# One program block from the merge of keys to the end, the loop's first image prepared amid the way back of positions, and 29 of 32 gather chunks ahead

## The reference, cut to what matters

```python
x = x + conv(_ln_c(x))            # x: (32, 64, 48, 48); 32 images of 2304 pixels, 64 channels
#   conv: s = relu(xn^T xn) ** 2 over the pixels of one image, out = s times a 1x1 projection g
t = _to_tokens(x)                 # 32 * 2304 = 73,728 tokens
t = t + ffn(_ln_t(t))
#   ffn, gates: h = x W_gat; edges (262,144) with random src, dst, and one loop edge for each token
#     e = leaky_relu(a_src[src] + a_dst[dst]);  softmax of e over the edges of each dst
#     agg[dst] = sum of alpha * h[src];  layernorm, mean over heads, top 2 of 4 experts
#   out = sum over experts of gate * (gelu(x W1 + b1) W2 + b2)
```

## Time and profile before

| what | us |
|---|---|
| median of 3 runs | 5424.05 |
| lowest and highest of them | 5416.19, 5426.34 |
| profiled execution, its own time | 5427.65 |
| its span from first to last instruction | 5425.8 |
| busy: PE, DVE, ACT, POOL | 3722.4, 3970.8, 3400.6, 2943.8 |

### The profile page before, as it was taken

How to read it: one execution, slowest core, us unless ns; L and a number is a source line. 1 busy time by engine, 2 the same in 40 slices (tenths; PEclk the granted TensorE clock), 3 DMA queues, 4 the chain that set the end, 5 groups by cost and what they waited for, 6 DMA issues and landing times.

```text
span 5425.8 us, 61836 instructions
## 1 busy us (share of the span) xinstructions
PE 3722.4 (69%) x18367; PEld 1256.6 (23%) x18367; DVE 3970.8 (73%) x5512; ACT 3400.6 (63%) x4285; POOL 2943.8 (54%) x2937
## 2 busy tenths in 40 slices
PE   4888988300499999999999999994000017777878
PEld 1223333100133333333333333331000002222222
DVE  8998988997466666666666655555888857777877
ACT  4777888202576767676676767674555536566666
POOL 6000000007777777777777777773777137666661
PEclk9999999655699999999999999996555558888889
DMA  7000100002112222222222222223555527999997
GB/s 264 23 24 20 29 20 21 11 16 59 36 39 58 45 55 53 48 53 47 56 45 54 54 47 50 46 45 103 176 170 168 188 71 144 142 162 155 154 166 139
DMA packets 332446, 441.38 MB, mean 81 GB/s; under 512 B 183193, under 2 KB 261916, under 8 KB 331500
## 3 DMA queue, kind: packets, MB, share of 16 engines
q1 hardware_dynamic: 209744, 288.12, 19.4%
q0 software_dynamic: 105536, 148.61, 16.5%
q10 hardware_dynamic: 16896, 1.18, 0.2%
HBM read 252.35 MB, written 166.47 MB: 77 GB/s over the span
## 4 chain that ended last, share of the span: by engine, by line
POOL 36%; issue 14%; DMA 14%; DVE 8%; PE 4%; ACT 1%; SPq 1%; DVEq 0%; POOLq 0%; ACTq 0%
POOL rows L1692 33%; DMA rows<-htab_d,idx 8%; DMA gs<-gates_d 4%; PE ye L1913 2%; PE up L1925 2%; DVE ms L2594 1%; POOL R L1750 1%; DMA gates_d<-GH 1%; DVE pairs L2601 1%; ACT GT L2087 1%; DVE AD L2460 1%; DVE AE L2454 1%; POOL got L1705 0%; DVE total L2603 0%; POOL nb L1707 0%
## 5 line engine op out<-in xcount | busy, mean ns | idle before, releaser
L1692 POOL DMA_INDIRECT rows<-htab_d,idx x2048 | 2135.1, 1043 | 802.0 <-issue 595.8
L2376 DVE SCALAR_TENSOR_TENSOR s<-gram,rel 128x1024 f32<-128x1024 f32 (+1 forms) x720 | 802.7, 1117 | 860.0 <-ACT rel L2042 850.3
L2042 ACT ACTIVATE rel<-gram 128x1024 f32<-128x1024 f32 (+1 forms) x1080 | 1009.6, 940 | 605.9 <-PE gram L1860 574.5
L1818 PE MATMUL acc<-s,gT 128*64 128x512 f32 (+1 forms) x4320 | 1075.3, 576 | 0.0
L1859 PE MATMUL gram<-hl 128*128 128x512 f16 (+1 forms) x2160 | 777.1, 365 | 117.9 <-DVE s L2376 93.1
L1860 PE MATMUL gram<-hl,lh 128*128 128x512 f16 (+1 forms) x2160 | 765.8, 360 | 0.0
L1750 POOL DMA_INDIRECT R<-seg_d,nidx x576 | 588.5, 1022 | 191.4 <-issue 165.8
L1913 PE MATMUL ye<-hid,w 128*64 128x384 f32 x1536 | 376.1, 569 | 273.0 <-DVE ms L2594 208.6
L1030 POOL IOTA slots<- 64x2048 int32 x1 | 1.8, 1833 | 975.4 <-POOLq L182 975.4
L2134 ACT ACTIVATE hid<-up,b1t 128x768 f32<-128x768 f32 x384 | 333.3, 899 | 269.3 <-PE up L1925 267.9
L1896 PE MATMUL tailsT<-ident,tails 128*20 128x128 f32 x24 | 5.3, 414 | 652.1 <-DVE tails L2482 652.1
(11 more groups left out here) (372 smaller groups left out, 5349.8 us busy)
## 6 DMA issues: line engine op xcount, KB each, us to landing
gs<-gates_d SPq DMA_DIRECT2D x64, 1024.0 KB
rows<-htab_d,idx POOLq DMA_INDIRECT x2048
seg_d<-state SPq DMA_DIRECT2D x32, 996.0 KB, 4.3
raw_d<-w_zeros POOLq DMA_DIRECT2D x48, 512.0 KB, 22.5
raw_d<-rows POOLq DMA_DIRECT2D x32, 768.0 KB, 3.6
tne<-tn_d SPq DMA_DIRECT2D x32, 576.0 KB, 6.6
x2e<-x_d SPq DMA_DIRECT2D x32, 576.0 KB, 9.8
out<-res SPq DMA_DIRECT2D x64, 256.0 KB
```

Source lines behind the costliest of these rows:

```text
L1692: pool.indirect_dma_start(out=n.rows[:, k % 2, j, :], out_offset=None, in_=n.htabx, in_offset=bass.IndirectOffsetOnAxis(ap=n.idx[:, g % 2, ...
L1818: last = pe.matmul(acc[(par + c) % 2][j * C:(j + 1) * C, 0:w], gT[:, par, 2 * k + j, :], s2[:, u % SLOTS, j * w:(j + 1) * w], start=k == 0 ...
L2042: act.activation(rel[:, t % RELS, 0:2 * w].rearrange("p (j x) -> p j x", j=2), gram[(par + t) % 2][:, :, 0:w], ACT.Relu, scale=1.0 / SPLIT ...
L2376: dve.scalar_tensor_tensor(halves(s2[:, t % SLOTS, 0:2 * w]), gram[(par + t) % 2][:, :, 0:w], 1.0 / SPLIT ** 2, halves(rel[:, t % RELS, 0: ...
```

## The change

- Merge and routing stand in one block: the five streams of `merge_nodes` become functions (`merge_sync` and so on) that `flow` calls first. The semaphores of POOL's gather become ones of the whole program.
- POOL's gather is a function of its own (`gather_rows`). Its first 48 gathers (`OPENING`) are issued in the merge stream, the others follow. SP loads the first two index tiles `idx` right behind the store of `gidx_d`. `need` is computed for each of the 32 chunks, not for 8 groups.
- `AHEAD` goes from 28 to 29 chunks and `PIECE` from 11 to 8.
- Image 8 is loaded, projected, scaled and transposed between steps 7 and 17 of the way back. The buffers that it uses come after a filler (`apart`, 48 KiB a partition), so that they don't lie on those of the routing; `routed` has three parts, not four.
- In the edge stage ACT raises `a_ends` behind `AE` and a new `a_got` behind `GT`; DVE waits for `a_got` ahead of the first use of `GT`, and POOL waits for `a_got`.
- POOL's subtraction on `pos` stands behind the last gather, not behind the repair scatter.

```diff
-    AHEAD = 28
-    PIECE = 11
-    EARLY = 10
-    IN_FLIGHT = 4
+    AHEAD = 29
+    PIECE = 8
...
+def gather_rows(pool, n, t0, t1):
+    GC, G, NK = n.GC, n.G, 4 * n.G
+    for t in range(t0, t1):
+        k, j = divmod(t, GC)
+        g, c = divmod(k, 4)
+        if j == 0:
+            need = pool.value_load(n.need[0:1, NK - 1 - k:NK - k], min_val=16, max_val=16 * n.B)
+            pool.wait_ge(n.o_hx, need)
+            pool.sem_inc(n.opened, 1)
+        if j == 0 and c == 0:
+            if g < 2:
+                pool.wait_ge(n.i_in[g], 16)
+            else:
+                pool.wait_ge(n.j_in[g % 2], 16 * (g // 2))
+        if j == 0 and k >= 2:
+            pool.wait_ge(n.raw_out[k % 2], 16 * (k // 2))
+        if t >= IN_FLIGHT:
+            pool.wait_ge(n.landed[t % IN_FLIGHT], 16 * (t // IN_FLIGHT))
+        pool.indirect_dma_start(out=n.rows[:, k % 2, j, :], out_offset=None, in_=n.htabx,
...
+        def merge_sync(sp):
             sp.wait_ge(v_ids, 1)
             sp.dma_start(n.gidx.rearrange("(p j) a -> p (j a)", p=P), big[0][:, 0, :].bitcast(I32)).then_inc(ids_out, 16)
+            sp.wait_ge(ids_out, 16)
+            for par in range(2):
+                sp.dma_start(n.idx[:, par, :, :], ids_of(n)[n.G - 1 - par]).then_inc(n.i_in[par], 16)
...
             pool.wait_ge(one_out, 16)
-
-        @block.tensor
-        def _(pe):
+            pool.wait_ge(v_need, 1)
+            gather_rows(pool, n, 0, OPENING)
...
         @block.sync
         def _(sp):
+            n.merge_sync(sp)
...
+            load(0, 0)
+            load(1, 1)
+            sp.wait_ge(n.a_hl, NTB * (FIRST + 1))
+            swap_halves(0)
             sp.sem_inc(moves_free, 1)
             sp.wait_ge(v_xpos, 1)
             sp.dma_start(n.xpos[0:n.M, :].rearrange("(p j) a -> p (j a)", p=NR), slots[0:NR, 0:EC]).then_inc(x_out, 16)
             sp.wait_ge(x_out, 16)
-            load(0, 0)
-            load(1, 1)
-            sp.wait_ge(n.a_hl, NTB * (FIRST + 1))
-            swap_halves(0)
...
             t = AHEAD * GC
-            gather(0, t)
+            gather_rows(pool, n, OPENING, t)
             pool.wait_ge(img_done, 1)
...
+            pool.wait_ge(p_in, 16)
+            pool.tensor_scalar(pos[:, :], pos[:, :], -1.0, 0.0, ALU.add, ALU.max).then_inc(n.m_rdy, 1)
             pool.wait_ge(v_fi, 1)
...
             pool.wait_ge(fix_out, 16 * G)
-            pool.wait_ge(p_in, 16)
-            pool.tensor_scalar(pos[:, :], pos[:, :], -1.0, 0.0, ALU.add, ALU.max).then_inc(n.m_rdy, 1)
...
                     last.then_inc(pe_route, 1)
-            pe.wait_ge(n.x_in[0], 64 * (FIRST // 2 + 1))
-            for i in range(NB):
-                pre(FIRST, 0, i)
-            for i in range(NTB):
-                turn(FIRST, i)
+                if turn_no == 0:
+                    pe.wait_ge(n.x_in[0], 64 * (FIRST // 2 + 1))
+                    for i in range(NB):
+                        pre(FIRST, 0, i)
+                if turn_no == 1:
+                    for i in range(NTB):
+                        turn(FIRST, i)
+            pe.wait_ge(a_route, routes_done[-1])
...
-                act.activation(AE[:, par, :, :], nb[:, par, :, HE + NH:HE + 2 * NH].rearrange("p j h -> p h j"), ACT.Copy)
-                act.activation(GT[:, par, :, :], got[:, par, ::-1, 0:HE + NH].rearrange("p j w -> p w j"), ACT.Copy).then_inc(a_ends, 1)
+                act.activation(AE[:, par, :, :], nb[:, par, :, HE + NH:HE + 2 * NH].rearrange("p j h -> p h j"), ACT.Copy).then_inc(a_ends, 1)
+                act.activation(GT[:, par, :, :], got[:, par, ::-1, 0:HE + NH].rearrange("p j w -> p w j"), ACT.Copy).then_inc(a_got, 1)
...
+                if i == 9:
+                    spread(FIRST)
+                if i == 11:
+                    scales(FIRST)
+                if i == 13:
+                    units(FIRST)
+                if i == 15:
+                    low(FIRST)
...
+                    dve.wait_ge(a_got, k + 1)
                     link(dve.tensor_tensor(ee[:, :, :], gt[:, HE:HE + NH, :], AD[:, :, 1:CE], ALU.add))
```

More of the change, by code:

```diff
@@ L28 @@
 MIRROR = 40959
+IN_FLIGHT = 4
+EARLY = 10
+OPENING = 48
+KEPT = 49152
 def chunks(n, size=512):
@@ L111, in kernel_program @@
         n.o_hx = sem("o_hx")
+        n.i_in = [sem("i_in0"), sem("i_in1")]
+        n.j_in = [sem("j_in0"), sem("j_in1")]
+        n.landed = [sem(f"landed{f}") for f in range(IN_FLIGHT)]
+        n.raw_out = [sem("raw_out0"), sem("raw_out1")]
+        n.opened = sem("opened")
         n.o_tn = sem("o_tn")
@@ L1260, in flow @@
         with ExitStack() as routing:
[L1261 to L1268, removed]
+            routed_ps = routing.enter_context(nc.psum_tensor("routed", [P, 3, 1024], F32))
         vr = im_sb("vr", [P, QT, C])
         gT = im_sb("gT", [P, 2, QT, C])
[L1271 to L1278, removed]
         rel = im_sb("rel", [P, RELS, 1024])
@@ L1294, in flow @@
         step_t = im_sb("step_t", [P, W], U8)
+        apart = im_sb("apart", [P, KEPT // 4])
+        xh = im_sb("xh", [P, 2, HALF])
+        cv = im_sb("cv", [P, QT, 2 * C])
+        sq = im_sb("sq", [P, QT, C])
+        tk = im_sb("tk", [P, QT, C])
+        tw = im_sb("tw", [P, QT, 2, C], F16)
+        hl = im_sb("hl", [P, 2, NP], F16)
+        lh = im_sb("lh", [P, 2, NP], F16)
+        ssq = im_sb("ssq", [P, QT])
+        sd = im_sb("sd", [P, QT])
+        r2 = im_sb("r2", [P, QT])
+        n2 = im_sb("n2", [P, QT])
+        rstd = im_sb("rstd", [P, QT])
+        nrm = im_sb("nrm", [P, QT])
+        rn = im_sb("rn", [P, QT])
+        scl = im_sb("scl", [P, QT])
         gram = [im_pb(f"gram{i}", [P, 2, 512]) for i in range(2)]
@@ L1664, in _ @@
         def _(pool):
+            n.merge_gpsimd(pool)
             pool.wait_ge(n.f_rdy, 1)
[L1667 to L1670, removed]
[L1671 to L1699 removed]
             def segment_rows(k):
@@ L2023, in _ @@
                 cn = nxt
+                if i == 8:
+                    for q in range(NB):
+                        pre(FIRST, q)
+                if i == 10:
+                    deviation(FIRST)
+                if i == 12:
+                    norm(FIRST)
+                if i == 14:
+                    high(FIRST)
+                if i == 16:
+                    for q in range(NTB):
+                        turned(FIRST, 0, q)
             evacuate("node_pos_back")
             evacuate("edge_pos")
-            for i in range(NB):
-                pre(FIRST, i)
-            deviation(FIRST)
-            norm(FIRST)
-            high(FIRST)
-            for i in range(NTB):
-                turned(FIRST, 0, i)
+            act.wait_ge(v_xpos, 1)
             def body(b, own, par, nth, before, more, moved=None):
```

162 lines of the change are left out of this document (70 added, 92 removed).

## The result

The changed kernel takes 5334.78 us (median of 4 runs, 5333.47 to 5346.97) against 5423.11 for the kernel before on the same chip (5416.19 to 5426.34). The ratio is 0.9844, with a 95% interval of 0.9826 to 0.9861. The forecast was 5342.

The account below looks back on a forecast made before the run. Bounds: a dependent chain at the hand-over, POOL's pace in 23 edge passes, ACT and DVE's in the last eight. Hand-over 27.7, edge stage 51.3 and `pos` 2.5 save 81.5: 5424.05 - 81.5 = 5342 us, range 5325 to 5375.

Parts of the forecast that it names:

- What bounds it: Hand-over: one dependent chain; edge stage: POOL's pace in the first 23 distances (20.34 us), ACT and DVE's 19.36 afterwards.
- Hand-over, the 38.0: Routing to image loop: of 41.2 us between `slots` and DVE's first `s`, 3.2 remain and 38.0 go.
- What comes in on the way back, 10.3: Way back: image 8's pieces lengthen it by 10.3 us (8 if they overlap better, 18 if no slack is usable).
- the four links: Way back, DVE: four small links of at most 0.27 in a long step without slack, +1.0 us.
- Gathers ahead: Merge to images' end: 60 gathers fit into the merge, all end at 3672, 30 us ahead of 3701.6; cost 0.
- The rival in which gathers hold DVE in the merge: Merge, 1124.5 to 1222: each of DVE's 106 instructions waits 0.94 for a gather, 100 us, 5442 us; slower has 0.04.
- the rule set beside it: Skill's SBUF rule: a two-input VectorE instruction and GpSimd lock a shared port pair; the second waits for all of it.
- Edge stage, 51.3: Edge passes: DVE and ACT set all 31 distances at 18.54, 3.3 saved in pass 0; 51.3 us saved (30 to 53).
- `pos`, 2.5: Between scatter and `nidx`: POOL does `pos` while the last passes run, 2.5 us saved (2.2 to 2.9).
- The sum: Whole kernel: 27.7 + 51.3 + 2.5 = 81.5 us saved, for a median of 5342 us.
- the signs of being wrong: `S` keeps distances over 19, POOL's wait for `img_done` is gone, or the loop's images take longer than before.
- the five faster cases: Forecast's own 0.72, edge passes at POOL's pace or half-way 0.09, late gathers 0.05, lost way back 0.07, faster than 5326 0.03.

Follow-up runs that it names:

- The first and the second edit of the edge stage: Changed kernel with 28 chunks ahead and pieces of 11: 5379.27 us; changed kernel with DVE's first instruction of a pass waiting for `GT` again: 5370.68 us.
- the finer pieces: Changed kernel with image 8's pieces laid out finer along the way back: 5331.36 us, ratio 0.9838; on another chip 5361.21 us, ratio 0.9841.
- the pieces of 4 and 6: Changed kernel with 30 chunks ahead and pieces of 4: 5376.27 us, ratio 0.9926; with pieces of 6: 5396.72 us, ratio 0.9904.

## Why the prediction was right

The mechanism held: each stretch changed by the wait that was named for it. What was off is what the hand-over is made of, and how many gathers fit into the merge.

*What bounds it.* It held: one chain at the hand-over, POOL's pace in 23 passes, ACT's `GT` in the others. The first and the second edit of the edge stage each bring back their own pace (20.1 and 19.37).

*Hand-over, the 38.0.* The size was right (38.1), but the prediction read the 41.2 us as image 8's preparation alone. It was 27.7 that the preparation takes when its input is there, 11.5 because of a load issued late (9.4 of waiting and 2.1 of a batch that could have run before), and 2.0 of `vr` and `gT` on the path. The wait stood in the trace, on PE ahead of the first `misc`. The forecast needed only the sum, so it was not hurt. But it could not have told what the early load is worth alone.

*What comes in on the way back, 10.3.* Measured 9.8, term by term as distances of ACT's copies: step 9 +5.1 (forecast 5.4), the sums +0.75 (0.8), the four links +0.8 (1.0), `units` +1.3 (1.35), `low` and the `hl` copies +1.6 (1.7), the end +0.2. That only what exceeds the slack of its engine lengthens the step is shown by the finer pieces, where ACT's parts fit into its slack.

*Gathers ahead.* The size was low: 72 gathers up to 1236.5, not 60, since beside the 0.68 us instructions a gather is hardly stretched. When the loop starts it was 170, not 157, which at 1.33 us each is 17 of the 25 us by which POOL was done earlier (3647, not 3672). It was idle for 53.7 us, not 30. The cost of 0 held. The rival in which gathers hold DVE in the merge is gone (149.59, 149.61 and 149.67 us). Of the rule set beside it only the half on POOL shows in the merge: DVE's instructions that came second did not wait.

*Edge stage, 51.3.* Measured 3.6 + 49.7 = 53.3, 0.3 above the range of 30 to 53. The pace is 18.48 (forecast 18.54). A pass of POOL was forecast at 15.8 to 16.6 us. The first five distances of `got` have a mean of 16.1, until POOL is so far ahead that it falls into DVE's 18.5, and the pieces of 4 and 6 go no faster than 18.4. So POOL has room.

*`pos`, 2.5.* Measured 2.7, and 2.35 when undone.

*The sum.* Without the mix and the 0.9 us ahead of the merge, the stretches save 83.4 us where 81.5 was forecast. That is 1.9 of the 7 us between 5342 and 5334.8. The other 5 come from stretches that the change does not touch, above all the mix, and are luck. The place where the merge starts is of that kind too: without a change ahead of it, it lies between 1070.1 and 1073.5 us in the profiles, and the 0.9 of the table is inside of that. The mix was 966.4 us in the profile of before and 957.2 in that of the change, 955.2 to 963.9 in eight more profiles on two chips, and 985.3 to 994.7 in three profiles on a third. The changed kernel itself gave 957.2 and 985.3, the latter far outside of the 955 to 966 that its second run was expected to give. So the mix's length varies with the execution and the chip. The kernel before was profiled only once, so its mix can't be compared on one chip. But the whole times speak against an effect of the change: for all eleven kernels of the experiments the medians save 1 to 7 us less than the trace has saved, against that of before, when `R` is first used (81.9 = 5449.08 - 5367.17 and 82.9 for the changed kernel on the third chip). Only in the first result they save 4 us more (88.3 and 84.3). What makes the mix's length vary is not settled; two rows of windows, over 500 us of the changed kernel's mix, on the chip of the first result and on the third of the experiments, show the DMA engines busy all the time at different rates (last two columns):

```profile
4616.00:5116.00 500.00, 400.54 (x1674) 117.38 (x1672) 401.97 (x989) 331.45 (x367) 323.42 (x329) 0.85 1.00 157
```

```profile
4616.00:5116.00 500.00, 377.69 (x1596) 111.00 (x1596) 386.36 (x948) 318.36 (x353) 309.69 (x317) 0.85 0.99 152
```

*The signs and the chances.* Of the signs of being wrong one came, but within what profiles differ: the loop's images took 1.0 us longer (2286.6 for 2285.6), and the same loop took 2285.6 to 2290.4 in the other kernels whose POOL was in time. The chances of the five faster cases add up to 0.96, where 0.95 is said beside 0.01 for the same time.

## What to carry to other kernels

Work that is laid into a tightly coupled loop of two engines costs what exceeds the idle time of its own engine in that step. So cut it into pieces of that size, and put the rest where the pair waits for a third engine. Before a latency chain is moved, look whether its head waits for a load that only stands in the wrong place of a queue: here that was over a quarter of the 41 us, with the batch that could then run early. Where two engines hold a pass in turn, undoing each alone shows two paces (20.1 and 19.4 us here), and only both edits together give the third (18.5). And when a share of work is moved ahead, check the points at which the code demands that all of it is done.

## What the runs showed of the hardware that I had not expected

- In these rows a gather is stretched by the length and the kind of the DVE instruction beside it, not by DVE's busy share: 1.97 us in every second one beside 1.22 us instructions with two inputs, 0.94 to 1.13 beside the 0.68 us ones, at a DVE that has no gaps in either stretch. Beside a TENSOR_REDUCE of 2.88 us (1258.94) and a MEMSET of 2.25 us gathers took 0.94 to 0.98. DVE's instructions in the merge did not change. One outside of it did: the routing's first CAST takes 1.53 us in the kernel before, and 1.58 to 1.70 in the seven profiles in which a gather had begun 0.59 to 0.71 us ahead of it (in the other five the gather was older or not there, and it took 1.53).

```profile
1234.43 0.94 POOL L980 DMA_INDIRECT rows<-htab_d,idx  x1 [0.30 <-issue]
1235.08 1.65 DVE L2210 CAST nodes<-edges 128x2624 int32<-128x2624 f32 x1 [13.53 <-DMA edges<-mkey_d]
```

- The image loop now starts on PE right behind the transposes. Its first eight `gram` products ran at a granted clock of 1.00 (2.4 GHz), the next ones, behind 2.93 us of idle time, at 0.50 (1.2 GHz), and from 1419.3 at 1.00 again. The loop's third `s` starts 7.09 us behind the first (1421.49 - 1414.40), where it was 5.41 before the change, and is 5.41 with image 8 behind the way back.

```profile
1407.50:1409.50 2.00, 1.90 (x8) 0.70 (x8) 1.93 (x1) 0.04 (x1) 1.70 (x2) 1.00 0.09 10
1412.40:1419.00 6.60, 5.20 (x12) 1.16 (x12) 4.08 (x4) 4.33 (x5) 5.10 (x5) 0.50 0.18 41
1419.30:1425.00 5.70, 5.70 (x26) 1.52 (x24) 2.45 (x2) 3.08 (x4) 4.45 (x5) 1.00 0.10 11
```

- Of the two images of one iteration of the loop, the first takes 93.9 to 94.2 us (from `hx` to `hx`), the second 95.9 to 98.5 in nine of eleven iterations, and how long it is differs from profile to profile. So the stretch from `s` to the images' end took 2285.6 to 2290.4 us in kernels whose loops are the same and whose POOL was in time. What makes the second image longer was not followed.
